# Second batch's expert layer: plain fp32 products on raw W1 tiles in place of a split into high and low parts

## The reference, cut to what matters

```python
logits = x @ W_router
expert_idx = jnp.argmax(logits, axis=-1)
h = jnp.einsum('th,ehi->tei', x, W1) + b1          # W1: 4 experts x 512 x 2048
h = jax.nn.gelu(h, approximate=False)
onehot = jax.nn.one_hot(expert_idx, E, dtype=x.dtype)
intermediate = jnp.einsum('te,tei->ti', onehot, h)
y = intermediate @ Wo + bo + x
y = _layer_norm(y, ln_gamma, ln_beta)
```

## Time and profile before

| | us |
|---|---|
| median of 3 runs | 566.1 |
| lowest and highest | 565.6, 566.4 |
| the profiled execution's own time | 568.86 |
| its span, first to last instruction | 566.8 |
| TensorE busy (matmul) | 530.3 |
| VectorE busy | 294.7 |
| ScalarE busy | 209.1 |

### The profile page before, as it was taken

The page is one execution under the profiler, slowest core; times in us unless marked ns, Lnnn a source line. Parts: engine busy times, 40 slices in busy tenths (PEclk is TensorE's granted clock), DMA queues, the critical chain, the costliest instruction groups (busy, mean ns, idle before and its releaser), DMA issues.

```text
span 566.8 us, 8877 instructions
## 1 busy us (share of the span) xinstructions
PE 530.3 (94%) x3582; PEld 373.3 (66%) x3582; DVE 294.7 (52%) x608; ACT 209.1 (37%) x305; POOL 37.2 (7%) x32
## 2 busy tenths in 40 slices
PE   7999999999998989999997999798999999799895
PEld 6777776777776668987765777455765446566542
DVE  3635535747574642461964766612384427855332
ACT  3110026464645323273225364452163126544300
POOL 0210000000691000000000000000000000000000
PEclk8999999999998999999997999899999999999998
DMA  8700000000630003221000000942966677774000
GB/s 278 298 0 1 1 1 0 2 2 2 223 149 1 2 9 124 91 76 41 18 1 0 1 2 9 419 169 69 418 264 213 233 270 261 269 288 148 2 19 19
DMA packets 11311, 62.22 MB, mean 110 GB/s; under 512 B 1540, under 2 KB 2564, under 8 KB 4484
## 3 DMA queue, kind: packets, MB, share of 16 engines
q1 hardware_dynamic: 11272, 61.66, 29.2%
HBM read 61.13 MB, written 0.52 MB: 109 GB/s over the span
## 4 chain that ended last, share of the span: by engine, by line
PE 87%; DVE 6%; ACT 3%; issue 2%; DMA 1%; SPq 0%; POOLq 0%; POOL 0%; DVEq 0%; ACTq 0%
PE ps L942 40%; PE ps L1003 11%; PE ps L1192 10%; PE ps L989 6%; PE ps L1018 5%; PE ps L1233 4%; PE ps L1216 2%; DVE w1L L916 2%; PE ps L1218 2%; PE ps L1217 2%; DVE Pm L590 1%; ACT w1H L525 1%; DMA raw<-in_ctxT 1%; PE ps L1201 1%; PE ps L936 1%
## 5 line engine op out<-in xcount | busy, mean ns | idle before, releaser
L359 ACT COPY PT<-ps 128x512 f32<-128x512 f32 x96 | 53.4, 589 | 103.7 <-PE ps L1003 103.7
L1003 PE MATMUL ps<-ident,Pm 128*128 128x128 f32 x512 | 69.0, 277 | 1.6 <-ACT PT L359 0.7
L590 DVE TENSOR_SCALAR_CACHE_REDUCE Pm<-ps,small 128x512 f32<-128x512 f32 x96 | 66.4, 747 | 7.4 <-PE ps L989 7.2
L1003 PEld LDWEIGHTS ps<-ident,Pm 128*128 128x128 f32 x512 | 56.7, 141 | 19.6 <-issue 15.8
L351 ACT ACTIVATE Pm<-Pm,small 128x2048 f32<-128x2048 f32 x32 | 64.2, 2008 | 14.2 <-DVE Pm L590 14.2
L1192 PE MATMUL ps<-w1raw,z 128*128 128x512 f32 x128 | 60.2, 620 | 3.3 <-DVE Pm L590 3.3
L942 PE MATMUL ps<-ctxH,wkH 128*128 128x512 f32 x124 | 52.9, 427 | 5.9 <-DVE u L735 3.4
L942 PE MATMUL ps<-wvH,ctxH 128*128 128x512 f32 x128 | 51.6, 403 | 0.0
L942 PE MATMUL ps<-ctxL,wkH 128*128 128x512 f32 x124 | 50.3, 406 | 0.0
L942 PE MATMUL ps<-wvL,ctxH 128*128 128x512 f32 x128 | 50.1, 391 | 0.0
L942 PE MATMUL ps<-ctxH,wkL 128*128 128x512 f32 x124 | 50.1, 404 | 0.0
(11 more groups left out here) (165 smaller groups left out, 717.9 us busy)
## 6 DMA issues: line engine op xcount, KB each, us to landing
w1raw<-in_W SPq DMA_DIRECT2D x32, 1024.0 KB, 4.8
raw<-in_ctxT SPq DMA_DIRECT2D x7, 1024.0 KB, 4.8
woF<-in_ffn_Wo SPq DMA_DIRECT2D x4, 1024.0 KB, 15.8
raw<-in_ctxT SPq DMA_DIRECT2D x2, 512.0 KB, 6.1
wv_raw<-in_xWv SPq DMA_DIRECT2D x2, 512.0 KB, 8.4
wq<-in_xWq SPq DMA_DIRECT2D x1, 1024.0 KB, 13.0
wS<-in_xWo SPq DMA_DIRECT2D x1, 1024.0 KB, 7.0
wS<-in_wq SPq DMA_DIRECT2D x1, 1024.0 KB, 4.8
```

Of the source, the lines that this page charges most:

```text
L359: act.copy(PT[:, c % 2, i, :, :].rearrange("p k t -> p (k t)"), ps[:, T_BANKS[i % 2], :]).then_inc(pt_act, 1)
L590: dve.tensor_scalar(Pm[:, i, c * CH:(c + 1) * CH], ps[:, i, :], -1.0, mx[:, p % 2, i, c - 1:c] if c else NOT_YET, ALU.mult, ALU.min, accum ...
L1003: last = pe.transpose(ps[:, T_BANKS[i % 2], j * P:(j + 1) * P], Pm[:, i, c * CH + j * P:c * CH + (j + 1) * P], ident[:])
```

## The change

The second batch's experts are computed as the first batch's are. The fp32 tokens `yT[1]` are masked into one copy `z1`, and each chunk of a raw W1 tile is multiplied by one plain fp32 matmul. The tiles `w1H`, `w1L`, `yTH`, `yTL`, `zH` and `zL` go, and with them 16 casts on ScalarE, 16 subtractions on VectorE, the split of the tokens, and four of the eight maskings. TensorE waits for a tile's load (`w1_in`) where it waited for the split. A slot is refilled when TensorE has finished its tile. On ScalarE and VectorE the hidden layer's steps for the first batch (`gelu`, `hidden_T`, `ffn_residual`) now follow each other with no split between them. TensorE's order of tiles and of the work between them stays.

```diff
-        yTH = at("yTH", [P, KT, T], F32R, 48)
-        yTL = at("yTL", [P, KT, T], F32R, 50)
-        zH = at("zH", [P, NW1, T], F32R, 32)
-        zL = at("zL", [P, NW1, T], F32R, 40)
+        z1 = at("z1", [P, NW1, T], F32, 32)
...
                 if r >= NW1:
-                    sp.wait_ge(w1_split, r - NW1 + 1)
+                    sp.wait_ge(w1_tile, r - NW1 + 1)
...
             transposed(yT[1], x2T_mm, 1, XT_BANKS[1], x2T_done)
-            transposed(yTH, x2T_mm, 1, XT_BANKS[1], yT_hi)
             masks(1)
-            for n in range(NW1):
-                k = NW1 + n
-                act.wait_ge(w1_in[k % RING], 16 * (k // RING + 1))
-                if n == 1:
-                    act.wait_ge(cT_dve[1], 2 * HPG)
-                if n >= 2:
-                    act.wait_ge(w1_tile, n - 1)
-                act.copy(w1H[n % 2][:], w1raw[k % RING][:]).then_inc(w1_hi, 1)
-                if n == 1:
-                    gelu(0)
-                if n == 3:
-                    hidden_T(0, 0)
-                    hidden_T(0, 2)
+            gelu(0)
+            hidden_T(0, 0)
+            hidden_T(0, 2)
...
-            dve.wait_ge(yT_hi, 1)
-            dve.tensor_tensor(yTL[:], split4(ps[:, XT_BANKS[1], :]), yTH[:].bitcast(F32), ALU.subtract).then_inc(yT_lo, 1)
             onehots_T(1)
             dve.wait_ge(mask_done, 2)
-            dve.wait_ge(yT_lo, 1)
...
-            masked_both(0)
-            for n in range(NW1):
-                dve.wait_ge(w1_hi, n + 1)
-                if n == 1:
-                    dve.wait_ge(o2_mm, 2)
-                if n >= 2:
-                    dve.wait_ge(w1_tile, n - 1)
-                dve.tensor_tensor(w1L[n % 2][:], w1raw[(NW1 + n) % RING][:], w1H[n % 2][:].bitcast(F32),
-                                  ALU.subtract).then_inc(w1_split, 1)
-                if n in (1, 2, 4):
-                    masked_both({1: 1, 2: 2, 4: 3}[n])
-                if n == 3:
-                    hidden_T(0, 1)
-                    hidden_T(0, 3)
-                if n == 5:
-                    ffn_residual(1)
+            for e in range(E):
+                masked(z1, yT[1][:], 1, e, z1_split)
+            hidden_T(0, 1)
+            hidden_T(0, 3)
+            ffn_residual(1)
             finish(0)
...
-                    pe.wait_ge(yT_lo, 1)
-                pe.wait_ge(z1_split, 2 * (n // KT + 1))
-                pe.wait_ge(w1_split, n + 1)
-                wH, wL = w1H[n % 2], w1L[n % 2]
+                pe.wait_ge(z1_split, n // KT + 1)
+                k = NW1 + n
+                pe.wait_ge(w1_in[k % RING], 16 * (k // RING + 1))
                 for c in range(IC):
-                    cc = slice(c * CH, (c + 1) * CH)
-                    dst = ps[:, 4 + c, :]
-                    pe.matmul(dst, zH[:, n, :], wH[:, cc], start=(n == 0), stop=False)
-                    pe.matmul(dst, zH[:, n, :], wL[:, cc], start=False, stop=False)
-                    last = pe.matmul(dst, zL[:, n, :], wH[:, cc], start=False, stop=False)
+                    last = pe.matmul(ps[:, 4 + c, :], z1[:, n, :], w1raw[k % RING][:, c * CH:(c + 1) * CH],
+                                     start=(n == 0), stop=False)
                 last.then_inc(w1_tile, 1)
```

More of the change, by code:

```diff
@@ L115, in perceiver_block @@
         z = at("z", [P, NW1, T], F32, 24)
-        yTH = at("yTH", [P, KT, T], F32R, 48)
-        yTL = at("yTL", [P, KT, T], F32R, 50)
-        zH = at("zH", [P, NW1, T], F32R, 32)
-        zL = at("zL", [P, NW1, T], F32R, 40)
+        z1 = at("z1", [P, NW1, T], F32, 32)
         RING = 4
         w1raw = [at(f"w1raw{i}", [P, I], F32, 64 + 8 * i) for i in range(RING)]
-        w1H = [at(f"w1H{i}", [P, I], F32R, 128 + 16 * i) for i in range(2)]
-        w1L = [at(f"w1L{i}", [P, I], F32R, 136 + 16 * i) for i in range(2)]
         b1raw = at("b1raw", [E, I], F32, 160)
@@ L215, in perceiver_block @@
         mask_mm, mask_done, ohT_mm, ohT_ready = sem("mask_mm"), sem("mask_done"), sem("ohT_mm"), sem("ohT_ready")
-        ones_ready, z0_done, yT_hi, yT_lo, z1_split = (
-            sem(n) for n in ("ones_ready", "z0_done", "yT_hi", "yT_lo", "z1_split"))
-        first_tile, w1_hi, w1_split, w1_tile = (sem(n) for n in ("first_tile", "w1_hi", "w1_split", "w1_tile"))
+        ones_ready, z0_done, z1_split = (sem(n) for n in ("ones_ready", "z0_done", "z1_split"))
+        first_tile, w1_tile = (sem(n) for n in ("first_tile", "w1_tile"))
         w1_mm, gelu_done, hT_mm, hT_act, hT_dve = each("w1_mm"), each("gelu_done"), each("hT_mm"), each("hT_act"), each("hT_dve")
@@ L897, in _ @@
             router(1)
-            dve.wait_ge(yT_hi, 1)
-            dve.tensor_tensor(yTL[:], split4(ps[:, XT_BANKS[1], :]), yTH[:].bitcast(F32), ALU.subtract).then_inc(yT_lo, 1)
             onehots_T(1)
             dve.wait_ge(mask_done, 2)
-            dve.wait_ge(yT_lo, 1)
-            def masked_both(e):
-                masked(zH, yTH[:].bitcast(F32), 1, e, z1_split)
-                masked(zL, yTL[:].bitcast(F32), 1, e, z1_split)
-            masked_both(0)
-            for n in range(NW1):
-                dve.wait_ge(w1_hi, n + 1)
-                if n == 1:
-                    dve.wait_ge(o2_mm, 2)
-                if n >= 2:
-                    dve.wait_ge(w1_tile, n - 1)
-                dve.tensor_tensor(w1L[n % 2][:], w1raw[(NW1 + n) % RING][:], w1H[n % 2][:].bitcast(F32),
-                                  ALU.subtract).then_inc(w1_split, 1)
-                if n in (1, 2, 4):
-                    masked_both({1: 1, 2: 2, 4: 3}[n])
-                if n == 3:
-                    hidden_T(0, 1)
-                    hidden_T(0, 3)
-                if n == 5:
-                    ffn_residual(1)
+            for e in range(E):
[3 more added lines that the diff above has]
+            ffn_residual(1)
             finish(0)
```

## The result

The changed kernel takes 572.1 us, the median of 4 runs (570.1 to 573.55), against 566.11 before. The ratio is 1.0104, with a 95% interval of 1.0073 to 1.0136. It is slower, as forecast, but by 6.0 us instead of 2.1, and outside the range. In two later series, on two chips, beside fresh runs of the kernel before, the ratio came out as 1.011 (1.0077 to 1.0144) and 1.0080 (1.0045 to 1.0116). The ratios leave out slow executions, those over 1.5% above the fastest of their kernel, while a median given without a remark is of all.

What follows compares the result with a forecast made beforehand. TensorE was taken to bound the kernel. Products 11.3 us dearer, less 9.3 us of stalls given back, plus 0.1 for changes of matmul kind, made 2.1 us slower: 566.1 to 568.2 us, range 567.0 to 569.8.

Steps and rivals of the forecast that it cites:

- The bound, and the stage: TensorE bounds; second batch's first product to its bias takes 61.51 us; removed VectorE and ScalarE work counts only where TensorE waits.
- Removed products and stalls: Second batch's tiles: 192 fp32r products, 43.6 us, go, and 9.3 us of waiting for the split and restarting.
- The estimate of 4.4 us: Second batch's tiles, from the skill's pass counts: 3.41 against 2.56 us a tile, stretch 4.4 us longer.
- Added products: Second batch's 16 tiles in plain fp32: 3.433 us each, 54.9 us; stretch to the second bias 2.0 us longer.
- Edits at nothing, and the loads: Token copy, subtraction and masks ahead of the second batch's tiles, and W1 loads within them: no cost or gain.
- a sign of being wrong: Start of the second batch's products: the prediction would be wrong if it were at another time than about 471.7.
- Behind the stage all moves by the same amount.: From the second bias to the kernel's end: work, order and the layer norm wait stay, keeping 33.6 us.
- The pace: Second batch's plain fp32 tiles run cheaper than in the first batch; below 3.31 us a tile, kernel faster; chance 2%.
- the loads didn't bind: W1 loads for the second batch become the bound, 576 us for one slow round of the ring; chance 4%.
- the unprofiled executions showed no longer stalls: Second batch's split waits are a tenth longer in unprofiled runs, cutting the price by 0.9 us, to 567.0; chance 12%.

Runs made afterwards that it cites:

- the pair without falls: The changed kernel and the kernel before, each with both batches' bias products at 128 rows instead of 4: 566.70 us and 565.91 us.
- the probe: Kernel before, both biases at 128 rows, extra products after its end: 4-row products lengthened 8 of 12 behind plain fp32, 12 of 12 behind fp32r; 128-row 0 of 6.
- the lengthened kernel before: Kernel before with ten more fp32r products, results unused, between its last tile and the second bias: 572.31 us, ratio 1.0097.

## Why the prediction was right or wrong

**The bound, and the stage.** Right. The removed work of VectorE and ScalarE brought nothing but the stalls.

**Removed products and stalls.** Right: 43.6 and 9.3 us. With a third pair of buffers the stage takes 53.2 us at full clock, where 43.6 + 8.6 is 52.2, so about 8.3 of the 9.3 us were waits for the split. The estimate of 4.4 us beside the prediction's sum is wrong in its working. The 9.3 us were found by subtracting the products, so a lower price for an fp32r product leaves more for the stalls by as much. The two together are 52.9 us at any price, and only the price of plain fp32 decides the difference.

**Added products.** Right. The four stretches of L1176 sum to 7.06 + 20.60 + 13.73 + 13.73 = 55.1 us; the forecast had 54.9 and 0.1 for changes of kind. The stage grew by 2.2 us in the first trace and by 2.3 in the pair without falls.

**Edits at nothing, and the loads.** Right. TensorE had no idle time in the stage, the landing times stayed at 4.7 to 17.9 us with a median of 4.8, and VectorE and ScalarE came out at 255.2 and 178.6 us. The stage began at 471.00 instead of about 471.7, which the prediction called a sign of being wrong. The second trace of the kernel before has it at 469.07, so this start moves between executions of one kernel.

**"Behind the stage all moves by the same amount."** Wrong, and this is the step that failed. From the start of the second bias to the end it was to stay 33.6 us; it took 571.8 - 534.75 = 37.0. I read the clock only in the windows of the stage, and only asked whether closing gaps could raise it. I had taken a TensorE that is busy for one that keeps its clock. The first trace couldn't show more, since both of its biases passed without a fall. But slices of the page at 8 tenths of the clock, and a mean clock of 0.975, 28 us at half clock in a span of 566.8, were a hint that the clock moves in this kernel. A term for it, 0 to 3.4 us on top, belonged in the range.

**Its size.** Of the 5.0 to 6.0 us, the stage is 2.2 to 2.3. The rest, some 3 us, is the clock: shown by the 4.7 us that 128 rows give back in the changed kernel, by the 1.7 or 3.3 us of a fall in the probe, and by the lengthened kernel before. The mean time at half clock bears this out. The changed kernel's executions have 4.2 us more of it, 5.5 by those that the ratios use. Of the changed kernel's, 1.0 us less lie at the very end, where TensorE has finished (3.6 against 4.6 in the first traces), so 5.2 to 6.5 us more lie where there is work. At the cost of a fall in dense work, half its length, that is 2.6 to 3.2 us (an estimate). With the stage's 2.3, less the 0.3 by which the time outside the span is shorter in the changed kernel (1.8 against 2.1, which no run explains), that makes 4.6 to 5.2 us. The means of the same executions differ by 4.5 and 5.1.

What isn't settled is how this time divides among the places. Most traces of both kernels have falls of 3.4 or 6.8 us elsewhere too, near 10, 173, 300 and 363 us, and not each in every execution. They move the total as the biases do.

**The rivals.** None was it. The pace didn't come down, the loads didn't bind, and the unprofiled executions showed no longer stalls. The rival that was missing is that a change of length has a price of its own for what stands behind it.

## What to carry to other kernels

A short run of matmuls with few contraction rows can be followed by half the clock for the dense work behind it although the engine is never idle; filling the rows with zeros cost TensorE nothing and removed it in 6 of 6 cases here, against 20 falls in 24 without. A change that only moves such a run may cost more than its own work (here 6.0 us for 2.3 of work), so read the granted clock behind the changed place too, in more than one execution. And where TensorE waits for a producer with two buffers, try a third before removing the producer. Here that took 8 us from the stage and 4.8 from the kernel's median, where dropping the split for plain fp32 took the stalls away and gave all back in products.

## What was not expected of the hardware

The fall of the clock with TensorE busy throughout: four 4-row products of 512 columns, 3.6 us in all, were followed by 3.4 or 6.8 us at 0.50 in the traces of the kernels, and by a loss of 1.7 or 3.3 us in 20 of 24 cases of the probe. Plain fp32 took 3.43 us for a tile of four products and fp32r 0.227 us a product, so three fp32r products cost 0.68 us against 0.86 for a plain one. An execution of the kernel before took from 562.8 to 576.2 us on the same chip, in step with its mean clock (0.993 to 0.967).
